# The second parts of q and k on GpSimd, and all first normalisations on VectorE

## The reference

```python
x = x + attn_a(layernorm(x))        # softmax(q k^T / sqrt(8)) v, then @ Wout + bout
x = x + ffn(layernorm(x))           # (silu(x Wg^T) * (x Wu^T)) Wd^T
x = x + attn_b(layernorm(x))        # the same with k_pos > q_pos masked
x = x + ffn(layernorm(x))
# layernorm(x) = (x - mean) / sqrt(var + 1e-5);  qkv = x @ Wqkv + bqkv
```

## Time and profile before

| | us |
|---|---|
| median of 3 runs (lowest, highest) | 1374.61 (1371.66, 1381.24) |
| the profiled execution | 1372.5 |
| its span, first to last instruction | 1370.7 |
| PE busy in it | 1322.5 (96%), mean granted clock 0.974 |
| DVE busy | 1180.1 (86%) |
| ACT busy | 1010.7 (74%) |
| POOL busy | 141.6 (10%), 309 instructions |
| chain of waits, share by engine | PE 83%, DVE 7%, ACT 5% |

### The profile page before, as it was taken

The page is one execution under the profiler, slowest core; times in us unless marked ns, Lnnn a source line. Parts: engine busy times, 40 slices in busy tenths (PEclk is TensorE's granted clock), DMA queues, the critical chain, the costliest instruction groups (busy, mean ns, idle before and its releaser), DMA issues.

```text
span 1370.7 us, 26878 instructions
## 1 busy us (share of the span) xinstructions
PE 1322.5 (96%) x9681; PEld 678.7 (50%) x9681; DVE 1180.1 (86%) x2979; ACT 1010.7 (74%) x1813; POOL 141.6 (10%) x309
## 2 busy tenths in 40 slices
PE   9899999999999999999997988999999999999898
PEld 6544444444444444444435764555555555555477
DVE  8799999999999999999935987788888888888376
ACT  8688888888888888888885542677677767777643
POOL 5620000000000000000001211100000000000011
PEclk9699999999999999999999996899999999999999
DMA  7611101111101111101000433121112211220001
GB/s 215 187 33 32 28 6 32 33 32 33 27 8 32 33 33 33 29 6 33 2 1 1 117 99 93 40 57 33 34 33 55 43 34 34 46 51 2 3 24 39
DMA packets 40060, 58.44 MB, mean 43 GB/s; under 512 B 7796, under 2 KB 19448, under 8 KB 39928
## 3 DMA queue, kind: packets, MB, share of 16 engines
q1 hardware_dynamic: 39928, 56.72, 17.2%
HBM read 36.77 MB, written 18.87 MB: 41 GB/s over the span
## 4 chain that ended last, share of the span: by engine, by line
PE 83%; DVE 7%; ACT 5%; issue 3%; SPq 1%; DMA 1%; POOL 0%; DVEq 0%; ACTq 0%; POOLq 0%
PE psum L1141 28%; PE psum L1077 24%; PE psum L1107 16%; ACT probs L630 4%; PE psum L1005 3%; PE psum L1228 3%; DVE maxima L859 3%; PE psum L1212 2%; PE psum L1115 2%; PE psum L1016 1%; DVE hid L935 1%; PE psum L1157 1%; PE psum L1054 1%; DVE junk L856 1%; PE psum L990 1%
## 5 line engine op out<-in xcount | busy, mean ns | idle before, releaser
L630 ACT ACTIVATE probs<-psum 128x512 f32<-128x512 f32 (+3 forms) x1408 | 833.8, 659 | 213.3 <-PE psum L1107 110.0
L859 DVE TENSOR_REDUCE maxima<-psum 128x1 f32<-128x512 f32 x1232 | 773.6, 682 | 31.5 <-PE psum L1077 25.8
L1077 PE MATMUL psum<-kop,qop 62*128 62x512 f32 (+3 forms) x1744 | 561.6, 437 | 7.0 <-DVE maxima L856 1.5
L1107 PE MATMUL psum<-qop,kop 64*128 64x512 f32 (+3 forms) x1792 | 525.1, 422 | 9.1 <-ACT probs L630 3.3
L1077 PEld LDWEIGHTS psum<-kop,qop 62*128 62x128 f32 x1744 | 267.0, 188 | 376.9 <-DVE maxima L859 285.2
L1141 PE MATMUL psum<-probs,v 128*32 128x512 f32 (+3 forms) x3584 | 440.4, 563 | 0.7 <-ACT probs L630 0.7
L1107 PEld LDWEIGHTS psum<-qop,kop 64*128 64x128 f32 x1792 | 268.3, 188 | 79.3 <-ACT probs L630 46.6
L856 DVE CUSTOM_DVE_ANT_0 junk<-psum,mask 128x384 bf16<-128x384 f32 (+3 forms) x512 | 232.1, 485 | 52.0 <-PE psum L1077 50.0
L1141 PEld LDWEIGHTS psum<-probs,v 128*32 128x32 f32 x3584 | 71.0, 109 | 100.9 <-issue 69.9
L1115 PE MATMUL psum<-half_ident,key_mask 64*128 64x64 bf16 x1024 | 89.0, 197 | 0.0
L523 POOL TENSOR_TENSOR att<-att_raw,rden 128x128 f32<-128x128 f32 x64 | 26.1, 407 | 511.2 <-DVE rden L888 511.2
(11 more groups left out here) (102 smaller groups left out, 749.0 us busy)
## 6 DMA issues: line engine op xcount, KB each, us to landing
qop<-q_parts SPq DMA_DIRECT2D x256, 64.0 KB
kop<-k_parts SPq DMA_DIRECT2D x64, 128.0 KB
kop<-k_parts SPq DMA_DIRECT2D x128, 64.0 KB
q_parts<-parts SPq DMA_DIRECT2D x24, 256.0 KB, 2.9
k_parts<-parts SPq DMA_DIRECT2D x24, 256.0 KB, 3.1
x<-in_L_attn_a_x SPq DMA_DIRECT2D x8, 256.0 KB, 4.5
q_parts<-att SPq DMA_DIRECT2D x8, 256.0 KB, 3.6
k_parts<-att SPq DMA_DIRECT2D x8, 256.0 KB, 3.7
```

The source lines that it names most:

```text
L630: nc.scalar.activation(probs[:, slot, heads[0] % 2:heads[-1] % 2 + 1, c0:], psum[:, bank:bank + len(heads), c0:], ACT.Exp, scale=SCORE_SCA ...
L859: nc.vector.tensor_reduce(dst, src, AX_X, ALU.max).then_inc(ring_free, 1)
L1077: mm(psum[:, bank, 0:width], qop[rows, buf, f, r, qb * P:(qb + 1) * P].bitcast(F32R), kop[rows, buf, r, kh * CHUNK:kh * CHUNK + width].bit ...
L1107: ins = mm(psum[:, bank + k, c0:], kop[rows, buf, c // 2, j * P:(j + 1) * P].bitcast(F32R), qop[rows, buf, f, c // 2, c0:].bitcast(F32R), ...
```

## The change

In both layers the second parts of chunks 0 to 6 are subtracted by GpSimd; chunk 7 stays on VectorE, which now also waits until the second part of the chunk before is done. In the first projection VectorE normalises all four tiles of each chunk and ScalarE none. GpSimd's `first_deviations` shrinks from four instructions to two, and the semaphore `xn_half_ready` goes. Semaphore and helper definitions that only lose a name are left out.

```diff
@@ GpSimd, first projection
             def first_deviations(n):
-                mean, var = first_moments[:, n, :, 0], first_moments[:, n, :, 1]
                 pool.wait_ge(first_moments_ready, n + 1)
-                nc.gpsimd.tensor_scalar(first_scale[:, 1, n], var, EPS, None, ALU.add).then_inc(first_steps, 1)
-                pool.wait_ge(first_steps, 3 * n + 1)
-                nc.gpsimd.tensor_tensor(first_scale[:, 0, n], first_scale[:, 1, n], power[:], ALU.pow).then_inc(first_steps, 1)
-                pool.wait_ge(first_steps, 3 * n + 2)
-                nc.gpsimd.tensor_tensor(first_scale[:, 1, n], mean, first_scale[:, 0, n], ALU.mult).then_inc(first_steps, 1)
-                pool.wait_ge(first_steps, 3 * n + 3)
-                nc.gpsimd.tensor_scalar(first_scale[:, 1, n], first_scale[:, 1, n], -1.0, None, ALU.mult).then_inc(first_scale_ready, 1)
-
-            for n in range(CHUNKS):
+                nc.gpsimd.tensor_scalar(first_scale[:, 1, n], first_moments[:, n, :, 1], EPS, None, ALU.add).then_inc(first_steps, 1)
+                pool.wait_ge(first_steps, n + 1)
+                nc.gpsimd.tensor_tensor(first_scale[:, 0, n], first_scale[:, 1, n], power[:], ALU.pow).then_inc(first_scale_ready, 1)
+
+            def split_parts(layer, n, buf):
+
+                pool.wait_ge(part1_ready, layer * CHUNKS + n + 1)
+                dst, p, earlier = parts_buffer(layer, n)
+                wait(pool, parts_stored[p], earlier)
+                nc.gpsimd.tensor_tensor(dst[:, 1], qk[:, buf], dst[:, 0], ALU.subtract).then_inc(part2_ready, 1)
+
+            for n in range(3):
                 first_deviations(n)
+            for n in range(CHUNKS - 1):
+                if n + 3 < CHUNKS:
+                    first_deviations(n + 3)
+                split_parts(0, n, n % 2)
@@ GpSimd, middle stage, end of a turn
                         inverse_deviation(0, moments[:, residual % 2], residual + 1)
+                    if qkv_rows is not None and qkv_rows < CHUNKS - 1:
+                        split_parts(1, qkv_rows, qkv_rows % 2)
@@ ScalarE, first projection
-            def normalise_first(n):
...
             def first_chunk(n, buf, m):
                 if m + 1 < CHUNKS:
                     copy_xt(n + 1, 1 - buf, 1 - buf)
-                if m + 2 < CHUNKS:
-                    normalise_first(n + 2)
                 take_qk(0, n, buf, 2 + 3 * buf)
@@ VectorE
                 dve.wait_ge(part1_ready, g + 1)
+                dve.wait_ge(part2_ready, g)
...
-            def normalise_second_half(n):
+            def normalise_first(n):
                 dve.wait_ge(first_scale_ready, n + 1)
                 wait(dve, xt_psum[0], n - 1)
-                for t in range(TPC // 2, TPC):
+                for t in range(TPC):
                     ins = nc.vector.tensor_scalar(xn[:, n % 2, t, :], x[:, n * TPC + t, :], first_moments[:, n, t, 0:1],
                                                   first_scale[:, 0, n, t:t + 1], ALU.subtract, ALU.mult)
-                ins.then_inc(xn_half_ready, 1)
+                ins.then_inc(xn_ready[0], 1)
...
                 add_v(0, n, buf, 4 + 3 * buf)
-                split_parts(0, n, buf)
+                if n == CHUNKS - 1:
+                    split_parts(0, n, buf)
...
-                        split_parts(1, qkv_rows, qkv_rows % 2)
+                        if qkv_rows == CHUNKS - 1:
+                            split_parts(1, qkv_rows, qkv_rows % 2)
```

More of the change, by code:

```diff
@@ L248, in transformer_pair_kernel @@
         rstd_ready = [sem(f"rstd_ready{k}") for k in range(2)]
-        xn_half_ready = sem("xn_half_ready")
         xn_ready = [sem(f"xn_ready{k}") for k in range(2)]
@@ L571, in take_biases @@
                 nc.scalar.copy(bvo[:, l].rearrange("p t e -> p (t e)"), psum[:, 7, 0:2 * E]).then_inc(setup_ready, 1)
-            def normalise_first(n):
[L574 to L579, removed]
             clear_query_rows(slice(0, 1), first_query_rows)
-            normalise_first(0)
             take_biases(0)
@@ L604, in _ @@
             copy_xt(0, 0, 0)
-            normalise_first(1)
             def first_chunk(n, buf, m):
@@ L814, in _ @@
             first_row_moments(1)
-            normalise_second_half(0)
+            normalise_first(0)
             first_row_moments(2)
-            normalise_second_half(1)
+            normalise_first(1)
             first_row_moments(3)
@@ L823, in first_chunk @@
                 if m + 2 < CHUNKS:
-                    normalise_second_half(n + 2)
+                    normalise_first(n + 2)
                 if m + 4 < CHUNKS:
@@ L1009, in transpose_xn @@
                 pe.wait_ge(xn_ready[0], g + 1)
-                pe.wait_ge(xn_half_ready, min(g + 1, CHUNKS))
                 transpose_tiles(xn[:, buf], bank).then_inc(xt_psum[0], 1)
```

## The result

The changed kernel took 1379.67 us, median of 20 runs (1374.93 to 1381.60), against 1373.99 us for 20 runs of the kernel before beside it. The ratio is 1.0031, 95% interval [1.0020, 1.0043]: slower by 4.3 us by that ratio, which holds runs of the same chip against each other (the bare medians differ by 5.7; one of the 20 runs of before took 2691.90 us and is not in the ratio), and inside the one per cent of the forecast. The forecast was 1381 us.

The account below looks back on a forecast made before the run. TensorE bounds the attention stages, the load-and-store chain the first projection's end, VectorE the middle-stage turns. Terms 3.4 + 1.8 + 2.3 = +7.5 us on 1373.5 gave 1381 us; 8-in-10 range 1369 to 1388.

Parts of the forecast that it names:

- The mechanism: Both layers: a VectorE normalisation starting beside GpSimd's subtraction is blocked for its whole rest, up to 2.44 us; chance 0.58.
- GpSimd's subtraction: Each of the 14 moved subtractions takes 2.44 us, the time of key_diff, with bounds of 1.2 and 3 us.
- First projection, +3.4 us: First projection: GpSimd's pace and held normalisations delay key_diff to 43.6 and the attention's first clip to 44.0, +3.4 us.
- the later normalisations: First projection: after chunk 3's held ones, normalisations fall in GpSimd's add and power, while the lag stays to chunk 7.
- Six turns, +1.8 us: Middle stage, chunks 0 to 5: the normalisation waits 1.4 us, gates come 0.3 us later per turn, +1.8 us.
- The seventh turn, +2.3 us: Middle stage: GpSimd holds the last chunk's normalisation, delaying TensorE's transposes and the jobs behind them by 2.3 us.
- The sum, +7.5 us: Whole kernel: 3.4 for the first projection, 1.8 for six turns and 2.3 for the seventh make +7.5 us.
- The level of before, 1373.5: Whole kernel: the unchanged kernel's time taken as 1373.5 us, the base to which the forecast's sum was added.
- no blocking (A): Normalisations run unheld: middle stage gains 4.6 us, first projection loses 1.0, so -3.6 us, 1370 us; chance 0.27.
- B: First projection: TensorE loses its clock before 35 us, 11.5 us more over chunks 3 to 7, 1393 us; chance 0.04.
- C: Normalisations beside GpSimd run at half pace, not blocked: +2 us, 1375 us; chance 0.11, shared with a cheap subtraction.

Follow-up runs that it names:

- middle_wait: Against the kernel before: only middle-stage subtractions of chunks 0 to 6 on GpSimd, each waiting for VectorE's next normalisation; ratio 0.9960, -4.5 us at equal clock.
- middle_six: Against the kernel before: only middle-stage subtractions of chunks 0 to 5 on GpSimd, chunks 6 and 7 on VectorE; ratio 1.0004, -0.5 us at equal clock.
- first_only: Against the changed kernel: layer 1's subtractions back on VectorE, leaving the change in the first projection alone; ratio to before 1.0014, +2.1 us at equal clock.
- middle_only: Against the kernel before: the change in the middle stage alone, first projection as before; ratio 1.0021, +1.6 us at equal clock.
- before_again: The kernel before, unchanged, profiled a second time; one run of 1372.30 us, span 1370.5 us.
- wait_six: As middle_wait, but chunk 6's middle-stage subtraction also stays on VectorE; ratio to the kernel before 0.9965, -5.0 us at equal clock.

## Why the prediction was right, and where not

**The mechanism** was right: where GpSimd's subtraction and VectorE's normalisation overlap, VectorE stands (1.11 us become 2.20, 3.14 and 3.24). A single held normalisation, 0.34 us alone, took 1.43, 2.38 and 2.47, and each ended 0.08 to 0.09 us behind GpSimd, whenever it had begun: it stands and is not merely slower. middle_wait is the proof that this is what costs. It changes only when GpSimd starts, the subtraction still takes 2.37 us beside VectorE's other work, and the gain is 6.1 us. The Trainium skill, "SBUF — State Buffer", section "Who interferes with whom", says that VectorE in a mode with both ports and GpSimd shut each other out, so that the one that issues later is blocked and not slowed, and that VectorE instructions with at most one SBUF input outside such a mode are free of it. The trace agrees with both, the second by add_v (0.85 us) and the gates (1.28). On who comes first it agrees where key_diff began well inside VectorE's subtraction (3.00 us in middle_six), but not in the seventh turn, where VectorE's start is recorded 0.05 us ahead and VectorE is held. There the measurement decides; whether so short a lead gives the true order isn't shown.

**GpSimd's subtraction** at 2.44 us: the fourteen took 2.34 to 2.40. The key_diff row that the price was taken from had itself been held: VectorE's subtraction (36.29, 1.23 us) ran beside its first 0.24 us, and without one key_diff takes 2.34 to 2.36.

**First projection, +3.4 us:** the start of the attention came 3.4 us later by the mean of the profiles. key_diff ended at 42.46, forecast 43.6; TensorE began at 42.61, forecast 43.6; the first clip came at 43.41, forecast 44.0. The detail is off by up to 1.1 us. GpSimd's pace was as forecast (3.7 to 3.9 us from chunk 0 to 5), but the seventh subtraction ended at 40.16 and not at 41.1. One step was wrong: the later normalisations didn't fall in GpSimd's add and power. In each of chunks 4 to 7 one met a subtraction and took 1.03 to 2.18 us in place of 0.34. At the end of the program +2.1 ± 0.5 is left at equal clock, which the forecast didn't foresee: it let every delay at the start of the attention pass through. About 0.5 of the 3.4 goes between 60 and 80 us, where the clock comes back sooner or later (see first_only). For the rest no stretch can be named, and it is hardly more than the interval.

**Six turns, +1.8 us:** this is the term that was mis-sized. Measured: -0.05 us each, -0.3 in all (shift +6.02 at 753 us, +5.74 at 820). The forecast let the normalisation stop for 1.4 us and then added its rest, with the gates at 4.67 us behind the start of the cast. They came at 4.31. The tile that was held had already been issued and ended with GpSimd (761.54, 1.43 us), so only three were left to do, and the gates began 0.78 us behind the subtraction (762.88 to 763.66) and not 1.04. The other 0.10 us is the subtraction's end, forecast 3.63 us behind the start of the cast and measured 3.53; it is a slip of the forecast's own sum, in which 776.6 and 2.44 make 779.04 and not 779.15.

**The seventh turn, +2.3 us:** TensorE's wait grew by 2.19 us (3.55 for 1.36), and the normalisations ended 2.14 later. At equal clock it is 2.1 (middle_six against middle_only). The shift in the profile after went from +5.75 to +8.65 at 836 us, but that includes the clock: from 839 us on it was +7.79. Right in place, kind and size.

**The sum, +7.5 us:** with the parts measured at equal clock, 2.1, -0.5 and 2.1, it would be 3.7. The difference is 3.1 at equal clock and 4.3 us by the ratio of the runs, so the sum was too high by 3.2 to 4.4, of which the six turns are 2.1 to 2.3 and the part of the first projection that didn't reach the end 1.3 (3.4 less 2.1). The one profile's shift at the end, 6.1, looks nearer to 7.5 and is no support for it: 2.7 of it came near 740 us (+3.3 to +6.0) with the fall of the clock that before_again has too, and from 857 us (+9.4) to the end 3.3 were given back. The level of before, 1373.5, was near its 1373.99. That 1381 lies only 1.3 above the median is in part luck: the bare medians differ by 5.7, more than either measure of the difference.

**Missed:** VectorE's last subtraction held by key_diff (3.17 us for 1.22). The cause was in the forecast, which asked it only of the normalisations. It delays GpSimd's cast L467 by 1.15 us and no row on the path that I found.

**The rivals:** no blocking (A) is out for this change, yet its price for the turns, 4.6 us, was close to the 4.87 that middle_wait gave. B is out: the granted clock was 1.00 in every 5 us up to 40 us of the profile after. It fell only at the start of the attention (0.71 in 40 to 45 us), just as in the profile before. C is out too, but by the rows alone, since VectorE's held instructions end with GpSimd's and are not stretched in proportion. By the total it isn't: its +2 us is nearer to the 3.1 at equal clock than the forecast's 7.5.

## What to carry to other kernels

Before work is given to GpSimd, list what VectorE does in those microseconds: here subtractions of two SBUF operands and tensor_scalar between SBUF tensors stood still for the length of GpSimd's subtraction, and those with an operand in PSUM did not. If work must go there, let it start behind the VectorE instruction that others wait for, with one wait: here a later start turned +1.6 us into -4.5. Where differences are under half a per cent, hold runs against each other at equal clock, and don't take one profile of before as its level.

## What the runs showed of the hardware

- GpSimd's subtraction of 128x1024 float32 numbers takes 2.34 to 2.40 us, VectorE's 1.22; a fill of the same size takes GpSimd 0.95 us.
- GpSimd is held too, when VectorE's subtraction is already running: key_diff took 3.00 us in middle_six, 2.76 in middle_only and 2.44 in before, with 0.78, 0.56 and 0.24 us of VectorE's subtraction left at its start, and 2.34 in wait_six with 0.04 left.
- A short lead does not protect VectorE: in the seventh turn its normalisation starts 0.05 us ahead by the record and is held for 2.47 us, while GpSimd takes its 2.34. With a lead of 0.15 us (15.14 against 15.29) the first normalisation ran in 0.34 us and the next one was held.
- A GpSimd instruction on few numbers holds nothing that can be seen: beside a power of 128x4 (19.45, 1.04 us, in before) VectorE's subtraction took its 1.22 us.
- One program differs between executions by up to 11 us (1370.4 to 1381.7 for the kernel before), and its mean granted clock, 0.967 to 0.977, goes with most of it: 0.90 us for 0.001, with 0.8 us of scatter left.
